# Writing out the last two attention steps and the start of the second feed-forward, and moving work from VectorE to GpSimd and ScalarE

## The reference

```
x = x + 0.5 * ffn(layernorm(x))
x = x + attn(layernorm(x))
x = x + 0.5 * ffn(layernorm(x))

attn: q = h @ wq.T (16 heads of 128), k, v = h @ wk.T, h @ wv.T (4 heads of 128)
      rotary embedding on q and k; k scaled by key_weights per query head
      softmax(q k^T / sqrt(128), causal) v, then @ wo.T

ffn:  logits = h @ router_w + router_b; top 2 of 8 experts, softmax over the two
      h_e = silu(h @ expert_w[e] + expert_b[e]) for all 8, weighted sum over e
      y = h + (sum @ proj_w + proj_b); out = norm_w * y / rms(y)
```

## Time and profile before

| | us |
|---|---|
| median of 3 runs | 811.82 (811.6 to 812.92) |
| the profiled execution | 813.12 |
| its span, first to last instruction | 811.3 |
| TensorE busy | 775.9 (96%) |
| VectorE busy | 632.7 (78%) |
| ScalarE busy | 534.4 (66%) |
| GpSimd busy | 512.3 (63%) |

### The profile page before, as it was taken

How to read it: one execution, slowest core, us unless ns; L and a number is a source line. 1 busy time by engine, 2 the same in 40 slices (tenths; PEclk the granted TensorE clock), 3 DMA queues, 4 the chain that set the end, 5 groups by cost and what they waited for, 6 DMA issues and landing times.

```text
span 811.3 us, 15659 instructions
## 1 busy us (share of the span) xinstructions
PE 775.9 (96%) x4520; PEld 676.7 (83%) x4520; DVE 632.7 (78%) x1888; ACT 534.4 (66%) x1314; POOL 512.3 (63%) x408
## 2 busy tenths in 40 slices
PE   7899999878999999999999999999999998999996
PEld 3688887757989989999999899899998986788885
DVE  6888996686777777777777777777777787988876
ACT  3555655777687777876777778767777674445543
POOL 4645739975877778778777777787877731112312
PEclk9999999898999999999999999999999999999998
DMA  9245321211132222212312312212212100000001
GB/s 297 76 153 194 113 98 40 56 36 24 33 89 65 52 53 62 55 40 77 91 26 50 99 32 78 78 39 52 78 40 50 40 1 1 0 1 27 6 22 52
DMA packets 30629, 50.11 MB, mean 62 GB/s; under 512 B 3970, under 2 KB 12802, under 8 KB 30594
## 3 DMA queue, kind: packets, MB, share of 16 engines
q1 hardware_dynamic: 30596, 49.71, 21.8%
HBM read 18.76 MB, written 9.96 MB: 35 GB/s over the span
## 4 chain that ended last, share of the span: by engine, by line
PE 79%; DVE 8%; POOL 6%; ACT 3%; issue 3%; DMA 1%; SPq 0%; POOLq 0%; DVEq 0%
PE pt L1802 8%; PE pj L1721 5%; PE pj L1723 5%; PE pj L1722 5%; PE o L1813 4%; PE o L1814 4%; PE o L1815 4%; PE sc L1789 4%; PE sc L1788 4%; PE sc L1787 4%; PE pj L1824 3%; PE pj L1826 3%; PE pj L1825 3%; PE sc L985 3%; PE sc L987 3%; PE sc L986 3%
## 5 line engine op out<-in xcount | busy, mean ns | idle before, releaser
L1605 ACT ACTIVATE at_pr<-at_pr,at_low 128x512 f32<-128x512 f32 (+7 forms) x256 | 135.0, 529 | 49.1 <-DVE at_low L1420 48.9
L1295 POOL TENSOR_TENSOR at_ql<-at_rot,at_qh 128x512 fp32r<-128x512 f32 x64 | 82.9, 1295 | 91.8 <-ACT at_qh L1564 91.7
L1420 DVE CUSTOM_DVE_ANT_0 at_pr<-sc,at_mask 128x512 f32<-128x512 f32 (+2 forms) x192 | 93.0, 521 | 59.7 <-PE sc L1789 59.7
L1614 ACT ACTIVATE at_pr<-at_pr,at_inv 128x512 f32<-128x512 f32 (+7 forms) x256 | 115.7, 524 | 12.4 <-DVE at_inv L1427 12.4
L1433 DVE CAST at_pth<-pt 128x512 fp32r<-128x512 f32 x192 | 106.3, 595 | 9.8 <-PE pt L1802 9.6
L1307 POOL TENSOR_TENSOR at_rot<-at_rot,gc 128x512 f32<-128x512 f32 x80 | 103.5, 1294 | 6.3
L1439 DVE TENSOR_TENSOR at_ptl<-pt,at_pth 128x512 fp32r<-128x512 f32 x192 | 105.1, 589 | 0.0
L1303 POOL TENSOR_TENSOR at_rot<-ga,cos 128x512 f32<-128x512 f32 x80 | 103.6, 1295 | 2.3 <-POOL at_ql L1295 2.3
L1305 POOL TENSOR_TENSOR gc<-gc,sin 128x512 f32<-128x512 f32 x80 | 103.5, 1294 | 1.0 <-DMA gc<-ga 1.0
L1802 PE MATMUL pt<-ident,at_pr 128*128 128x128 f32 x640 | 87.8, 276 | 6.0 <-DVE at_ptl L1439 3.1
L1802 PEld LDWEIGHTS pt<-ident,at_pr 128*128 128x128 f32 x640 | 76.0, 142 | 13.7 <-issue 5.3
(11 more groups left out here) (279 smaller groups left out, 2207.0 us busy)
## 6 DMA issues: line engine op xcount, KB each, us to landing
gc<-ga SPq DMA_DIRECT2D x160, 128.0 KB, 2.3
ga<-in_attn_w SPq DMA_DIRECT2D x8, 384.0 KB, 5.0
at_wo<-attn_split SPq DMA_DIRECT2D x6, 512.0 KB, 4.1
attn_split<-gb SPq DMA_DIRECT2D x6, 384.0 KB, 2.4
attn_split<-gc SPq DMA_DIRECT2D x6, 384.0 KB, 3.3
gb<-attn_split SPq DMA_DIRECT2D x6, 384.0 KB, 3.4
x<-in_x SPq DMA_DIRECT2D x4, 512.0 KB, 9.1
e_raw<-in_expert_w SPq DMA_DIRECT2D x8, 256.0 KB, 6.0
```

What stands on the lines that cost most here:

```text
L1605: act.activation(a, a, ACT.Exp, bias=low[kind][:, k:k + 1], scale=-1.0, accum_out=tot[kind][:, k:k + 1]).then_inc(ex_done, 1)
L1614: act.activation(a, a, ACT.Copy, scale=inv[kind][:, k:k + 1]).then_inc(nm_done, 1)
```

## The change

Behind TensorE's loop the two calls of `step` are replaced by written lists, on all four engines. VectorE's loop now ends with step 13 and GpSimd's with step 14. `feed_forward` hands out its functions at the start of the attention (`yield router, logits_back, experts` and the like) and the lists call them. Beside the new order these things change:

- the rows of sequence 0 are scaled by GpSimd (`norm_rows_last`), their statistics are taken in step 14, and their two column halves are transposed apart, both into bank sc[0];
- the rests of all four weight pairs are made by GpSimd (`pair_rest`);
- GpSimd's rotation of step 15 is taken apart into `cosine`, `sine` and `total`;
- the leads of the last four probability fills (units 2 and 3 of step 15) are made by ScalarE (`prob_lead_last`);
- the output product of step 15 is cut by pairs of heads for both halves (`output_last`): heads 0 and 1 are summed before, heads 2 and 3 behind, in the same bank, and x is added to twice.

```diff
 def gpsimd(pool, tail, second):
+            def norm_rows_last():
+                b, _ = NORMS[2]
+                pool.wait_ge(rstd_done, 3)
+                pool.wait_ge(tz_done, C * 2)
+                for t in range(BT):
+                    pool.tensor_scalar(z[:, t, :], x[:, b * BT + t, :], mv[:, 2, t, 0:1], rs[:, 2, t:t + 1],
+                                       ALU.subtract, ALU.mult).then_inc(z_done, 1)
+            def first_pair_rest():
+                hi, lo = first_pair(gb, wa_all)
+                pool.wait_ge(early, 1)
+                pool.wait_ge(raw_done, NR * last + 3)
+                pair_rest(0, hi, lo)
...
-            with pool.Fori(2, STEPS) as s:
+            with pool.Fori(2, last) as s:
                 rest(s - 1, NR - 1)
                 rope(s)
-            rest(STEPS - 1, NR - 1)
+            rest(last - 1, NR - 1)
+            cosine(last, 0) sine(last, 0) total(last, 0) sine(last, 1) sine(last, 2)
+            rest(last, 0) cosine(last, 1) cosine(last, 2) total(last, 1) total(last, 2)
             rstd(2)
+            rest(last, 1) cosine(last, 3) rest(last, 2) norm_rows_last()
+            cosine(last, 4) sine(last, 3) sine(last, 4) total(last, 3) total(last, 4)
+            rest(last, 3) rest(last, 4)
+            first_pair_rest() residual(0) pair_rest(1) pair_rest(2) next_rstd(1) pair_rest(3)
...
 def vector(dve, tail, second):     (from unit 0 of step 15 on)
+            mask_min(last, 2, (0, 1, 2))
+            prob_lead(last, 0, 3) inverse(last, 1, 0) inverse(last, 1, 1) out_rest(last - 1, 3)
+            inverse(last, 2, 0) prob_rest(last, 0, 2) prob_rest(last, 0, 3) mask_min(last, 2, (3,))
+            mask_min(last, 3, (0, 1, 2))
+            inverse(last, 2, 1) add_output(last - 1, 1) prob_lead(last, 1, 0) z_rest(2, 0)
+            mask_min(last, 3, (3,)) inverse(last, 3, 0)
+            prob_lead(last, 1, 1) prob_rest(last, 1, 0) prob_rest(last, 1, 1) out_rest(last, 0)
+            add_output(last - 1, 0) prob_lead(last, 2, 0) inverse(last, 3, 1) prob_rest(last, 2, 0)
+            prob_lead(last, 2, 1) prob_rest(last, 2, 1) out_rest(last, 1)
+            prob_rest(last, 2, 2, True) prob_rest(last, 2, 3, True) z_rest(2, 1) next_stats(1)
+            prob_rest(last, 3, 0, True) prob_rest(last, 3, 1, True) out_rest(last, 2)
+            choose_gap(0) choose_index(0) out_rest(last, 3) add_output(last, 1)
+            weigh_chosen(0) add_output(last, 0)
...
 def scalar(act, tail, second):     (the last part)
+            def prob_lead_last(u, k):
+                kind = u % 2
+                act.wait_ge(pt_ready, fill(last, u, k) + 1)
+                cols = slice(k * SEQ, k * SEQ + FLEN[kind][k])
+                act.activation(pth[kind][:, cols], pt[k % 2][:, 0:FLEN[kind][k]], ACT.Copy).then_inc(hi_last, 1)
...
+            exps(last, 3, (0,)) z_lead(2, 0) exps(last, 3, (1, 2)) out_lead(last, 0)
+            normalise(last, 2, (1, 2, 3)) normalise(last, 3, (0, 1)) exps(last, 3, (3,))
+            first_pair_lead() out_lead(last, 1) prob_lead_last(2, 2) prob_lead_last(2, 3)
+            normalise(last, 3, (2, 3)) z_lead(2, 1) prob_lead_last(3, 0) prob_lead_last(3, 1)
+            pair_lead(1) out_lead(last, 2) logits_out(0) silu_table() out_lead(last, 3)
+            half_tanh(0) pair_lead(2)
...
 def tensor(pe, tail, second):
+            def output_last(half, pair):
+                pe.wait_ge(ol_done, OL0 + unit(last, 2 * pair + 1 - half) + 1)
+                if pair == 0:
+                    pe.wait_ge(xu_done, 2 * (last - 1) + 2 - half)
+                for t in range(2):
+                    tok = slice((2 * half + t) * P, (2 * half + t + 1) * P)
+                    o = pj[1 - half][:, t * D:(t + 1) * D]
+                    for h in range(2 * pair, 2 * pair + 2):
+                        pe.matmul(o, oh[:, h, tok], wo[0][:, h, :], start=(t == 0 and h == 0), stop=False)
+                        pe.matmul(o, oh[:, h, tok], wo[1][:, h, :], start=False, stop=False)
+                        r = pe.matmul(o, ol[:, h, tok], wo[0][:, h, :], start=False, stop=(t == 1 and h == G - 1))
+                if pair == 1:
+                    r.then_inc(pj_ready, 1)
...
-            step(STEPS - 2, False, 1)
-            step(last, False, 0)
+            scores(last - 1, 2, (0, 1, 2)) output_late(last - 2) query(last, 2)
+            transpose_p(last - 1, 1, (0, 1)) scores(last - 1, 2, (3,)) scores(last - 1, 3, (0, 1))
+            weigh(last - 1, 0) scores(last - 1, 3, (2, 3)) transpose_p(last - 1, 2, (0, 1))
+            output_early(last - 2, False) transpose_p(last - 1, 2, (2, 3)) weigh(last - 1, 1)
+            query(last, 3) scores(last, 0, (0, 1)) transpose_p(last - 1, 3, (0, 1))
+            scores(last, 0, (2, 3)) scores(last, 1, (0, 1)) weigh(last - 1, 2)
+            scores(last, 1, (2, 3)) value(last) transpose_p(last, 0, (0, 1)) weigh(last - 1, 3)
+            value_T(last, False) transpose_p(last, 0, (2, 3)) scores(last, 2, (0, 1, 2))
+            output_late(last - 1) scores(last, 2, (3,)) transpose_p(last, 1, (0, 1))
+            scores(last, 3, (0, 1)) transpose_z(2, 0) scores(last, 3, (2,)) weigh(last, 0)
+            scores(last, 3, (3,)) output_early(last - 1, True) transpose_p(last, 2, (0, 1))
+            weigh(last, 1) output_last(1, 0) transpose_p(last, 2, (2, 3)) transpose_z(2, 1)
+            output_last(0, 0) transpose_p(last, 3, (0, 1)) weigh(last, 2)
             pe.wait_ge(zlo_done, C * len(NORMS))
-            router()
-            output(last, 1, pj[0])
-            router()
-            output(last, 0, pt[0], range(2, G))
+            router(0) experts(0, 0, 0, (0,)) logits_back(0) weigh(last, 3)
+            output_last(1, 1) experts(0, 0, 0, (1,)) output_last(0, 1)
...
 def body(i):                       (feed_forward, vector)
-                if i == 0:
+                if first and i == 0:
                     pair_rest(3)
```

More of the change, by code:

```diff
@@ L1317, in rope @@
                     rotate(s, r)
-            last_block = BATCH - 1
+            last_block, last = BATCH - 1, STEPS - 1
             rotate(0, 0)
@@ L1816, in weigh, with output @@
                 r.then_inc(o_ready, 1)
-            def output(s, half, bank, heads=range(G)):
+            def output(s, half, bank):
                 pe.wait_ge(wo_in, 32 * (s // BATCH) + WO0)
@@ L1840, in output_early, with step @@
                 output(s, 0, pj[1 if last else 0])
-            def step(s, first, ahead):
+            def step(s, first):
                 for u in range(UNITS):
@@ L1846, in step @@
                     s2, u2 = following(s, u, 2)
[L1847 to L1848 removed]
+                    if u == 2 and not first:
                         query(s + 1, 3)
[L1850 to L1851 removed]
+                    scores(s2, u2, range(BT) if u % 2 else range(BT - 1))
                     if u == 0 and first:
@@ L1920, in attention @@
-        return (wo, mask, mask_in, xu_done, rotated_lead, rows_normed), offsets, (sync, gpsimd, vector, scalar, tensor)
+            step(0, True)
+            with pe.Fori(1, last - 1) as s:
+                step(s, False)
+            scores(last - 1, 2, (0, 1, 2))
+            output_late(last - 2)
+            query(last, 2)
+            transpose_p(last - 1, 1, (0, 1))
+            scores(last - 1, 2, (3,))
+            scores(last - 1, 3, (0, 1))
+            weigh(last - 1, 0)
+            scores(last - 1, 3, (2, 3))
@@ new lines, in tensor @@
+            transpose_p(last - 1, 2, (0, 1))
+            output_early(last - 2, False)
+            transpose_p(last - 1, 2, (2, 3))
+            weigh(last - 1, 1)
+            query(last, 3)
+            scores(last, 0, (0, 1))
+            transpose_p(last - 1, 3, (0, 1))
+            scores(last, 0, (2, 3))
+            scores(last, 1, (0, 1))
+            weigh(last - 1, 2)
+            scores(last, 1, (2, 3))
+            value(last)
+            transpose_p(last, 0, (0, 1))
+            weigh(last - 1, 3)
@@ L1980, in _ @@
         def _(pool):
-            step_programs[1](pool, next(one[1](pool)))
-            for _ in two[1](pool):
+            second = two[1](pool)
+            step_programs[1](pool, next(one[1](pool)), next(second))
+            for _ in second:
                 pass
@@ L1988, in _ @@
             second = two[2](dve)
-            step_programs[2](dve, next(one[2](dve)), lambda: next(second))
+            step_programs[2](dve, next(one[2](dve)), next(second))
             for _ in second:
@@ L1995, in _ @@
             second = two[3](act)
-            step_programs[3](act, next(one[3](act)), lambda: next(second))
+            step_programs[3](act, next(one[3](act)), next(second))
             for _ in second:
@@ L2002, in _ @@
             second = two[4](pe)
-            step_programs[4](pe, next(one[4](pe)), lambda: next(second))
+            step_programs[4](pe, next(one[4](pe)), next(second))
             for _ in second:
```

559 lines of the change are left out of this document (355 added, 204 removed).

## The result

| | before | after |
|---|---|---|
| median, us | 812.37 (811.6 to 813.22, 4 runs) | 806.91 (806.07 to 807.47, 4 runs) |
| the profiled execution, span | 813.12, 811.3 | 807.34, 805.5 |

The ratio is 0.9927, 95% interval 0.9912 to 0.9943: 5.5 us faster by the medians, 5.8 by the spans. Forecast were 7.1 us and 804.7; the measured 806.9 lies within the forecast's own range of 802.6 to 807.4, close to its upper end.

The account below looks back on a forecast made before the run. TensorE was taken to bound the kernel, with VectorE the late engine for some 60 us in the rewritten stretch. 6.8 + 1.9 - 1.5, less 0.1, gave 7.1 us off 811.8: 804.7, own range 802.6 to 807.4.

Parts of the forecast that it names:

- The floor and the bound: Rewritten stretch to the third expert product: TensorE's unchanged work 57.6 us of 67.0, VectorE late; at most 11.3 winnable.
- Up to the scores of (15,2): Written order to the last step's middle: wait at 655.34 goes, TensorE there at 656.6 against 658.05, 1.5 us won.
- the scaling: Sequence 0's rows on GpSimd between rests of queries 2 and 3, step 15: 3.4 us for four, hidden behind the swap's transfer.
- the margin of 4.1: Time the four row scalings on GpSimd may take, 3.4 + 0.7, before the scores of (15,2) are held up.
- Rival 4: Row scaling on GpSimd holds the last rotation, TensorE waits before the scores of (15,2): slower, 815.0 us; chance 8%.
- The new wait in VectorE's list: Masked minimum of (15,3) waits 2.5 us for chunk 1's scores; TensorE then waits about 1.3; about 2 given back.
- The output product: Last output by pairs of heads covers the waits of 683.76 and 686.15, no gap; gain to third expert product 6.8.
- The relief of VectorE: Weight rests, row scaling, four casts and one output addition leave VectorE: 9.6 us in some 65.
- The weight rests: On GpSimd, 2.4 us each, pair 3 done at 693.7, 0.3 early; the waits at 697.77 and 702.90 go, 1.9 won.
- GpSimd beside VectorE: Pair 2's rest meets the chosen weights' products, pair 3's the scaling of block 1's rows; 1.5 charged of 4.1 us.
- Rival 1: VectorE and GpSimd block each other fully, and the gap at 669 drops the clock: 808.9 us; chance 18%.
- rivals 2 to 4: Everything fits, 800.5, 5%; late inputs merely move, 811.8, 7%; GpSimd's scaling holds the last rotation, 815.0, 8%.

Follow-up runs that it names:

- both edits: Changed kernel with chunk 1's scores issued with chunk 2's and the fourth weight pair's lead earlier, the fastest kernel: 802.92 us, 0.9888 of the kernel before.
- the earlier lead: Changed kernel with ScalarE making the fourth weight pair's lead one activation earlier: 804.62 us, ratio 0.9911 to the kernel before.
- the order-alone kernel: Changed kernel with rests, scaling and last casts back on VectorE and the last output product not split: 812.14 us, ratio 0.9998 to the kernel before.
- the kernel with the output whole: Changed kernel with the last output product not split by pairs of heads: 810.47 us, ratio 0.9978 to the kernel before.

## Why the prediction was right, point by point

*The floor and the bound.* Right. TensorE's work priced start to start at 57.6 us up to the third expert product, and waits on VectorE on top; with both edits it comes within 1.7 us of floor and what follows (57.6 - 1.9 for the first scores, + 9.2 to the router, which is the 11.1 before less the 1.9 of the two waits: 64.9). That the loop runs without a gap is so (TensorE is busy 227.00 of the 227 us from 400 to 627), but the earlier trace rows begin where the loop ends and do not show it.

*Up to the scores of (15,2).* Forecast 656.6, measured 657.29, less the 0.28 by which this trace is late: 657.0. The mis-sized term is the scaling: 3.4 was taken, 4.87 measured, over the margin of 4.1 by 0.8. By that margin it would cost 0.8; it cost 0.3. The six transposes before these scores start at 656.44 and cost 0.57 elsewhere (627.35 to 627.92), so the scores could have started at 657.01; they started at 657.29, right behind the end of GpSimd's rest at 657.24. At 1.22 each the scaling is outside the 0.7 to 1.0 that were forecast, and over the 1 us that was named, together with a wait of TensorE for at_ql, as a sign of being wrong. Rival 4's mechanism was there, at 0.3 us.

*The new wait in VectorE's list.* Forecast 2.5 and then 1.3 of TensorE, measured 2.48 and 1.25; about 2 given back with filling, measured by its removal 1.8.

*The output product.* No gap from weighing (15,2) on, as forecast. But the prediction gave the split no price of its own, only "cover". Its price is 2.4 us in the changed kernel and 75.7 - 71.1 = 4.5 without the moved work, counted for both quarters, the one that the kernel before had included. The relief of VectorE, which stood first in the argument as 9.6 us of its time (9.0 of it the moved work, 0.6 the addition that the output in two pieces saves), is worth 71.1 - 69.9 = 1.2 for the moved work beside the split and 75.7 - 72.3 = 3.4 without it.

*The weight rests.* 2.40 each, as forecast, pair 3 done at 694.56 against 693.7. The 1.9 of the two later waits less 1.5 for the blocking should leave 0.4; from the third expert product to the router it took 705.75 - 694.65 = 11.10 before and 699.80 - 688.84 = 10.96 after: 0.1.

*GpSimd beside VectorE.* Both collisions took place, where the working put them. VectorE lost 1.9 at L472 and 2.1 at L427; TensorE, by the earlier lead, 1.6. The size of the 1.5 charged stands, its split between the two does not, and that is luck: in the fastest kernel L472 still takes 2.12 and TensorE has no wait behind it, so the first collision costs TensorE nothing there, and the 1.6 came back by moving the second alone. Whether in the changed kernel the first also made the second worse was not separated. By the Trainium skill ("SBUF — State Buffer", "Who interferes with whom") the engine that comes first keeps the shared ports for its whole instruction. L472 and L463 agree: instructions of 32 and 8 columns, held for 2.12 and 2.04 us.

*The sum.* 7.1 forecast, 6.2 in the stretch: 0.7 late at the third expert product (0.3 of it the scaling; the other 0.4 was not traced to a term), 0.3 behind it. The spans differ by 5.8, because the list began 0.28 later and 0.1 was lost behind the router. By the medians it is 5.5 (an interval of 4.6 to 7.1). Rival 1 had its collisions but not its clock; the numbers of rivals 2 to 4 are not what came, though 0.3 us of rival 4 is in the trace. The place-2 wait and the blocking were in the forecast as costs, and both turned out to be edits of a line: had the text asked what removes them, it would have named 803.

## What to carry to other kernels

When two lists of instructions are walked against each other, look for the work that depends on nothing new, and put it where the late inputs are: half an output product placed there was worth 2.4 us beside the moved work and 4.5 without it, more than taking 9 us off the late engine (1.2 and 3.4). Price such measures with and without each other before calling one the large part. A wait on a semaphore that counts two results at once waits for the later; issue both before anything long. When work is moved to GpSimd, look at what VectorE does beside it with all operands in SBUF, down to the smallest instruction: a cast of 8 columns was held for 2.04 us here, while the probability rests, which read a bank of TensorE's results, were not.

## What was not expected of the hardware

Moving 5.7 us of subtractions from VectorE to GpSimd, with nothing else placed anew, shortened the stretch by only 0.7 us together with the scaling of sequence 0: four of TensorE's earlier waits stayed, and a 0.17 us cast and a 1.38 us scaling took 2.04 and 3.45 beside the moved work. And in the order-alone kernel, after waits of 0.61, 0.67 and 2.48 us TensorE's granted clock was 0.53 over the next 3 us, its lower level (1.2 GHz) for most of them, while in the kernel with the output whole, after 0.60, 0.67, 0.56 and 0.53 in about the same places, it stayed at the upper level (2.4 GHz) in the profiled execution.
